# A two-layer gated transformer-like kernel on one core: loads behind the feature stores, an earlier bias split, VectorE steps in another order, and a longer run of filler products

## What is computed

```python
x = x + tanh(g_xattn[0]) * gat2(ctx_512, layernorm(x), W0, a0, b0, W1, a1, b1)
x = x + tanh(g_ffn[0])   * ((silu(n @ gate_w.T * gate_s) * (n @ up_w.T * up_s)) @ down_w.T * down_s)   # n = layernorm(x)
x = x + tanh(g_xattn[1]) * ((1 - gamma) * layernorm(x) + gamma * sym(sigmoid(sim) * top_k_mask(sim)))
x = x + tanh(g_ffn[1])   * sum_over_top2(coef * w2 @ (silu(w1 @ n) * (w3 @ n)))
```

## Time and profile before

| | |
|---|---|
| median of 3 runs | 235.6 us (232.43, 235.60, 235.95) |
| the profiled execution | 235.69 us |
| its span, first to last instruction | 233.9 us |
| mean granted clock of PE, share of full | 0.969 |
| PE busy | 214.0 us, 92% |
| PE weight loads | 164.0 us, 70% |
| VectorE (DVE) busy | 131.9 us, 56% |
| ScalarE (ACT) busy | 85.5 us, 37% |
| POOL busy | 77.8 us, 33% |
| moved by DMA | 26.11 MB |

### The profile page before, as it was taken

One profiled execution on the slowest core, in us unless ns is written; L12 is line 12 of the kernel. 1 busy time (PEld: TensorE's weight loads), 2 busy tenths in 40 slices (PEclk: granted clock), 3 DMA queues, 4 the chain that ended last, 5 costly groups with the idle time before them and its releaser, 6 DMA issues.

```text
span 233.9 us, 3846 instructions
## 1 busy us (share of the span) xinstructions
PE 214.0 (92%) x1290; PEld 164.0 (70%) x1291; DVE 131.9 (56%) x462; ACT 85.5 (37%) x184; POOL 77.8 (33%) x106
## 2 busy tenths in 40 slices
PE   8899979999899979999989999999999999999920
PEld 7486754444487535988969998999999999544510
DVE  0768793758997996898798395851111111536300
ACT  1965434987600246222533245222222222333210
POOL 7704313061001130026450342554456443244320
PEclk9999977999999999999999999999999999999985
DMA  5777229525991014916243223122233312222110
GB/s 143 228 282 234 64 94 332 207 76 218 399 415 62 0 45 135 337 36 198 77 123 118 27 24 34 33 43 45 42 49 93 53 22 30 35 34 34 25 14 7
DMA packets 16107, 26.11 MB, mean 112 GB/s; under 512 B 3894, under 2 KB 11572, under 8 KB 16086
## 3 DMA queue, kind: packets, MB, share of 16 engines
q1 hardware_dynamic: 10774, 19.82, 23.7%
q0 software_dynamic: 3936, 5.64, 13.5%
q10 hardware_dynamic: 1376, 0.39, 0.7%
HBM read 20.73 MB, written 5.51 MB: 112 GB/s over the span
## 4 chain that ended last, share of the span: by engine, by line
PE 60%; DVE 20%; issue 6%; DMA 4%; POOL 3%; ACT 3%; DVEq 0%; POOLq 0%; ACTq 0%
PE PS L2023 21%; PE PS L2047 10%; PE PS L1904 6%; PE PS L1918 5%; PE PS L2063 3%; PE PS L2080 3%; DMA e<-graph_rows,gix 2%; DVE hT L1400 2%; POOL e L648 2%; PE PS L1731 2%; DVE stat L1025 2%; DMA graph_rows<-e 2%; PE PS L1753 2%; PE PS L2056 1%; PE PS L1963 1%
## 5 line engine op out<-in xcount | busy, mean ns | idle before, releaser
L2023 PE MATMUL PS<-hT,e 128*128 128x128 f32 x480 | 58.8, 276 | 0.8 <-ACT hT L931 0.8
L2023 PEld LDWEIGHTS PS<-hT,e 128*128 128x128 f32 x480 | 56.8, 192 | 2.2 <-ACT hT L931 1.5
L1904 PE MATMUL PS<-xnT,e 128*128 128x512 f32 x88 | 40.9, 613 | 2.4 <-DVE hT L1400 1.3
L1651 DVE TENSOR_TENSOR hT<-th,PS 128x512 f32<-128x512 f32 x18 | 12.4, 686 | 45.8 <-PE PS L2023 38.2
L1904 PEld LDWEIGHTS PS<-xnT,e 128*128 128x128 f32 x88 | 16.6, 196 | 22.4 <-issue 19.0
L2047 PE MATMUL PS<-e,hT 128*128 128x256 f32 x120 | 28.6, 381 | 0.2 <-DVE x L1438 0.2
L2047 PEld LDWEIGHTS PS<-e,hT 128*128 128x128 f32 x120 | 21.7, 190 | 3.1 <-issue 0.8
L1918 PE MATMUL PS<-e,hT 128*128 128x256 f32 x96 | 21.9, 383 | 0.0
L687 POOL DMA_INDIRECT out_dram<-a,ids_early x8 | 12.6, 1578 | 27.1 <-ACT a L960 18.0
L632 POOL TENSOR_TENSOR rstd<-veps,nhalf 128x2 f32<-128x2 f32 (+1 forms) x10 | 8.3, 827 | 35.6 <-DVE veps L1034 35.6
L1918 PEld LDWEIGHTS PS<-e,hT 128*128 128x128 f32 x96 | 17.9, 190 | 2.7 <-issue 0.5
(11 more groups left out here) (302 smaller groups left out, 352.7 us busy)
## 6 DMA issues: line engine op xcount, KB each, us to landing
e<-e_in SPq DMA_DIRECT2D x24, 512.0 KB, 6.3
x<-x_in SPq DMA_DIRECT2D x2, 512.0 KB, 5.6
graph_rows<-e SPq DMA_DIRECT2D x4, 256.0 KB, 3.0
out_dram<-x SPq DMA_DIRECT2D x4, 256.0 KB, 2.5
xn_rows<-xn SPq DMA_DIRECT2D x4, 256.0 KB, 2.3
e<-gw_in SPq DMA_DIRECT2D x1, 768.0 KB
e<-uw_in SPq DMA_DIRECT2D x1, 640.0 KB
e<-dw_in SPq DMA_DIRECT2D x1, 640.0 KB
```

Of the source, the lines that this page charges most:

```text
L1651: dve.tensor_tensor(hh[me], th[:, me, :], PS[:, 2 + me, :], ALU.mult).then_inc(gated, 1)
L1904: mm = pe.matmul(PS[:, bank, :], w[:, k, it * P:(it + 1) * P], xnT[:, h, k, :], start=(k == 0), stop=(k == 1))
L2023: mm = pe.matmul(PS[:, bank + q, f * P:(f + 1) * P], w[:, k * F + f * P:k * F + (f + 1) * P], xgT[q][:, k, :], start=(k == 0), stop=(k == 1))
```

## The change

Four edits, in the order of the program:

1. PE_ORDER: the filler between sims(0) and turn_ffn(0) has 13 products in place of 6.
2. DVE_ORDER: hidden_elu(1), which stood whole behind index(0), is cut in its two blocks; one stands between feat_elu(0, 0) and feat_elu(0, 1), the other behind feat_elu(0, 1), ahead of index(0).
3. SP: the transfers of gw, uw, gs and us leave the place ahead of the feature stores and are issued behind the first two of the four stores, just ahead of dw and dsr.
4. POOL: the six instructions of the bias split, with their wait for the bias load, stand ahead of the last constants (from Os on) and no longer behind them. The wait of PE for all constants moves from feat(0, 0) to hot(0), two steps later on PE.

```diff
-                    ("graph_check", 0), ("sims", 0), ("stay_warm", 6, 0), ("turn_ffn", 0), ("turn_ffn", 1), ("sims", 1),
+                    ("graph_check", 0), ("sims", 0), ("stay_warm", 13, 0), ("turn_ffn", 0), ("turn_ffn", 1), ("sims", 1),
...
-            for w, src in ((gw, gw_in), (uw, uw_in)):
-                sp.dma_start(w[:, :, :], src.rearrange("(k p) n -> p k n", p=P)).then_inc(ffn_loaded, 16)
-            for v, src in ((gs, gs_in), (us, us_in)):
-                sp.dma_start(v[:, :], src).then_inc(ffn_loaded, 16)
...
+            def load_up():
+                for w, src in ((gw, gw_in), (uw, uw_in)):
+                    sp.dma_start(w[:, :, :], src.rearrange("(k p) n -> p k n", p=P)).then_inc(ffn_loaded, 16)
+                for v, src in ((gs, gs_in), (us, us_in)):
+                    sp.dma_start(v[:, :], src).then_inc(ffn_loaded, 16)
...
             for b in range(B):
                 if b == 2:
+                    load_up()
                     load_down()
...
             pool.iota(iota_b[:, :], [[1, NL]], base=0, channel_multiplier=0, **small).then_inc(consts, 1)
+            pool.wait_ge(bias_loaded, 16)
+            own(pool.tensor_copy(bias_parts[:, :], bias[:, :]))
+            own(pool.tensor_tensor(bias_rest[:, :], bias[:, :], bias_parts[:, :], ALU.subtract))
+            own(pool.tensor_copy(bias_parts[32:64, :], bias_rest[32:64, :]))
+            own(pool.tensor_copy(bias_parts[64:P, :], bias_rest[64:P, :]))
+            own(pool.tensor_tensor(bias_rest[64:P, :], bias_rest[64:P, :], bias_parts[64:P, :], ALU.subtract))
+            own(pool.tensor_copy(bias_parts[64:P, :], bias_rest[64:P, :]))
+            pool.sem_inc(bias_ready)
             pool.memset(Os[:, :, :, 0:HT - 1], 0.0).then_inc(consts, 1)
...
             pool.wait_ge(consts, CONSTS)
-            pool.wait_ge(bias_loaded, 16)
...
-            pool.tensor_copy(bias_parts[64:P, :], bias_rest[64:P, :]).then_inc(bias_ready, 1)
...
-            def hidden_elu(h):
+            def hidden_elu(h, *parts):
-                for k in range(2):
+                for k in parts or range(2):
...
                 if h == 0 and p == 0:
-                    pe.wait_ge(consts, CONSTS)
...
             def graph_hot(h):
+                if h == 0:
+                    pe.wait_ge(consts, CONSTS)
```

More of the change, by code:

```diff
@@ L432, in build @@
                      ("silu", 5), ("copy_x", 6), ("scale_y", 4), ("silu", 6), ("copy_x", 7), ("scale_y", 5)]
-        DVE_ORDER = [("hidden_elu", 0), ("top", 0), ("hot", 0), ("top", 1), ("feat_elu", 0, 0), ("feat_elu", 0, 1), ("index", 0), ("hidden_elu", 1),
+        DVE_ORDER = [("hidden_elu", 0), ("top", 0), ("hot", 0), ("top", 1), ("feat_elu", 0, 0), ("hidden_elu", 1, 0), ("feat_elu", 0, 1), ("hidden_elu", 1, 1), ("index", 0),
                      ("lead", 0), ("scales", 0), ("flag", 0), ("graph_check", 0),
```

## The result

The changed kernel takes 239.97 us (median of four runs, 239.26 to 241.44), the kernel before 234.01 us beside it (232.17 to 235.95): ratio 1.029, interval 1.017 to 1.041 (the two medians by themselves give 1.025). It is slower, and 3.5 us above the top of the stated range of 231.0 to 236.5; whether by more than 2%, the interval leaves open. The ratios, and the medians from experiment 7 on, leave out every run over 1.5% above its kernel's fastest: single runs that lose another 5 us or so, whatever the cause (238.56 and 238.73 in experiment 8 are such, with a low clock in spite of the filler), and in some lists also runs of the kernel before at 235.2 to 236, so that the ratios of different experiments do not have quite the same base.

The account below looks back on a forecast made before the run. PE was taken as the bound, slowed by a half-clock stretch after a 1.95 us wait for xn. From 235.69 us: -3.3 (clock) + 0.2 (last row later) = 232.6, stated as 232.5; range 231.0 to 236.5.

Parts of the forecast that it names:

- contention term: Last of the four row gathers, now beside the moved loads: 0.6 us slower than its 2.78 us in quiet.
- The FFN loads behind the first two stores: SP's queue: first store lands sooner, gathers start at 19.5 (gain 0.4 us), loads hidden from PE, last row at 27.1.
- rival 2: Loads hold up the gathers: last takes 4.66 us, PE's gap 2.3 us, clock falls; 237.1 us; chance 0.11.
- upper bound of 1.9: Most the loads could add to the last gather, from the first gather's at most 4.66 us beside dw.
- Filler: PE before xn: 13 products (3.47 us) shrink the 1.95 us gap, clock stays full; gain 3.3 us, bounds 0 to 3.3.
- Rival 1: Clock falls all the same: a gap of about 1 us is enough or never the cause; 235.9 us; chance 0.15.
- Bias split: POOL: split ends at 9.2, constants at 11.1, first exponential at 13.3 instead of 12.57, first store issued 0.5 us later.
- VectorE steps: hidden_elu(1) halves ahead of index: gix at 18.65 instead of 17.72, second half's h0T 1.3 us earlier.
- First store: Feature store issued at 15.1, landing in 2.5 to 3.0 us, before gix, so gathers are held by gix.
- FFN loads in time: Loads and gathers, 2.8 MB, end at 28.6 to 30; PE asks at about 32: hidden, 2 us to spare.
- The later part: Everything behind the 31 to 45 us stretch moves along; second-half gathers 3 us earlier than 46.72.
- rival 3: Gathers start when the first store lands, not with gix, 1.7 us earlier with full clock: 230.7 us; chance 0.07.

Follow-up runs that it names:

- experiment 7: Kernel before with 13 filler products and the bias split ahead of the last constants, nothing else: 232.27 us (nine runs, 231.56 to 232.94).
- experiment 8: Kernel before with 13 filler products and the two VectorE steps moved, nothing else: 232.10 us (eight runs, 231.46 to 232.54).
- experiment 3: Kernel before with only the filler changed, 13 products in place of 6: 232.49 us, ratio 0.996.
- experiment 1: Changed kernel with gw, uw, gs and us loaded in their old place, ahead of the feature stores: 231.96 us, ratio 0.994.
- experiment 4: Changed kernel with 28 filler products in place of 13: 234.83 us (234.43 to 235.22).
- experiment 10: Changed kernel with 28 filler products and gw alone (0.79 MB) back ahead of the feature stores: 234.44 us, ratio 1.010.
- experiment 5: Changed kernel, but SP issues the FFN loads only when the four gathered tiles have landed: 240.77 us, ratio 1.037.
- experiment 6: Changed kernel with gw and uw loaded in pieces of 256 columns, 1 KB a row of one packet: 240.19 us, ratio 1.036.

## Why the prediction was wrong

The step that failed is the contention term in "The FFN loads behind the first two stores": "I take 0.6, a third of the way". Measured, the last gather took 6.19 us, 3.4 more than 2.78. The mechanism was named (rival 2); the term for it was mis-sized. The upper bound of 1.9 was wrong as well. It came from the first gather of before, which ran beside dw alone, 0.85 MB, when the change put 2.29 MB there. A bound from a row holds only for the load that the row had. The prediction's own sum stood against its 27.1 as well: it had loads and gathers together, 2.8 MB, end at 28.6 to 30, and in the trace the last bytes of the loads move before 29 and the gathers' before 30.

Point by point:

- **Filler.** Right in mechanism and size: alone it leaves one of two groups of runs, whose medians are 3.3 us apart (3.3 forecast), with the clock full. The four products of sims(1) take 1.99 us in experiment 3, as forecast. 13 products took 3.17 us, not 3.47. In the changed kernel the gap is 3.62 us and the filler saves nothing. Rival 1, that the clock falls anyway, is refuted where the gap is 0 to 0.62 us (the profiles of experiments 1, 3, 4, 7, 8 and 10). No run had a gap near the 1.1 us that the forecast expected for the whole change, so whether the clock would have held there was not tried; the forecast took it for granted.
- **Bias split.** The load was there at 5.06 (5.6 forecast), the split ended at 8.42 (9.2) and the last constant at 10.56 (11.1). ScalarE's sum started at 10.60 instead of 9.95, but the profile shows no wait before it: all of ScalarE's work was 0.46 us later in this execution and ended at 10.52. The forecast mechanism is seen in experiment 1, at about half its size:

```profile
10.80 1.06 ACT L794 ACTIVATE hT<-ctxT 64x1024 f32<-64x1024 f32 x1 [0.65 <-POOL node L619]
```

  No time could be measured for it.
- **VectorE steps.** gix at 18.99 (18.65 forecast) and the order of the steps as forecast. Worth nothing measurable.
- **First store.** Issued at 15.80 (15.1), landed in 2.5 us as forecast, and the gathers were released by gix and not by the store, as forecast, at 20.12 (19.5). The front varies from execution to execution: experiments 4, 5 and 6, with the same code up to the first two stores, issue the first gather at 19.30, 19.01 and 19.79, and the changed kernel at 20.12. In its profiled execution one step of hidden_elu on VectorE took 1.13 us at 8.86, beside POOL's last constants (the split had ended at 8.42), against 0.56 before; in experiment 4 the same step in the same place took 0.42, so neither the split nor the constants explain it.
- **FFN loads in time.** Right: PE never waited for them in the changed kernel. They were hidden from PE; their harm went to a transfer on another queue.
- **The later part.** Right: in the second half the gathers, with no such loads beside them, land in 2.76 us, and everything from there to the end is merely shifted.

The arithmetic closes in the profiled executions of experiment 1 (231.70) and the changed kernel (239.69), 7.99 us apart. The first gather is 0.67 later (20.12 against 19.45), the last takes 3.36 longer (6.19 against 2.83), so xn and turn_ffn are 4.02 later (34.44 against 30.42). By the next bf16 products (45.09 against 37.02) this has grown to 8.07, so the low clock cost 4.05 us. From the forecast: 232.5 + 2.8 (contention) + 0.6 (first gather) + 4.0 (clock) = 239.9.

Rival 2 was the right case. Its place, its mechanism and its point of decision (a gap above 1.95 us) all held; it was priced at 237.1 from the same too narrow bound, and given 0.11. The missing 2.6 us are about 2.1 of a later last row (30.5 instead of 28.4) and 0.7 of a clock that cost 4.05 us and not 3.3. The error is multiplied, since one term decides whether another one falls due: a last row that is later by 3.4 us loses 4 more through the clock. Such a term should have been carried to both sides, with the weight of its uncertainty. In rival 3 the start of 14.85 is neither the 14.61 of before nor the forecast's own 15.1; with 15.1 that case is worth 1.4 us and 231.0. The gathers did not follow the store, so nothing hangs on it.

Two rules of the Trainium skill were weighed. DMA: Bandwidth & Descriptors, "Queues, rings and completion order", has the engines serve their rings in turn; by it a gather should lose a fraction of a microsecond. That size was my own working, for which the section gives no time, and the traces do not bear it out: the first gather's bytes came about 2 us after they were due, and experiment 6, with packets of 1 KB, still took 7.0 us for the last. From 24 us on gathers and loads do move side by side (0.15 MB and 0.57 MB until 26). I leaned on the rule against a row, and that was the wrong way round. What in the path of the gathers holds them (the engines' turns, a queue of descriptors ahead of them, or memory) the runs do not show; they show that the last one pays for the bytes of the loads. TensorE: Matmul & The Clock Gate, "Why this matters for your kernels", asks only for longer gaps to be avoided. Here a gap of 1.95 us came before a fall in the profiled run of the kernel before, whose runs split about evenly between the two levels of time, and filler in that gap removed the split.

What stays open: why the loads alone (238.4 to 238.7) are 1.4 us quicker than the whole change, when they lack the filler. It rests on two runs against four; nothing here tells whether part of it is the front, which varies by 1.1 us between executions.

The version to keep is experiment 1: filler, bias split and VectorE steps, with the loads in their old place, 231.96 us (231.70 to 232.40). It beats the changed kernel by 8.0 us; beside before it is within the noise by the ratio, and lies in the quicker of before's two groups (231.67 to 232.43) with every run. Nearly all of what it gains is the filler; beside the filler alone, measured together with it, it is 0.5 us lower (232.33 to 232.65 there), which the two parts by themselves do not show.

## What to carry to other kernels

Before loads are moved to where "the queue is empty", list every small transfer of every other queue that lands in their shadow and that someone waits for, and price it at the volume that the move puts beside it over the engines' full rate (here 1.44 MB at 415 GB/s = 3.5 us, measured 3.1 to 3.4), not at a share of its own size. Look at the queues one by one, in the kernel as it is, for a stretch in which the small one moves nothing. A bound taken from a row is a bound only for the traffic that stood beside that row. And where a fall of the clock follows a wait of PE, fill the wait with spare products first (here about 3 us in every second run) and then keep the gap short, because a gap of 3.62 us brought the fall back in spite of the filler and cost 4 us on top of the delay.

## What the runs showed of the hardware

- Gathers on POOL's queue issued at 20.12 to 22.99, beside 2.29 MB of loads on SP's queue, moved no byte before 24 us, and the first was due about 2 us earlier; with no loads beside them (experiment 5) all four land within 3.1 us.
- Splitting the loads into packets of 1 KB brought the first gather's rows 5.2 us after its issue instead of 6.3 and did not help the last (7.00 us).
- The clock as against the gap that PE had before, where the gap is read from one profile for each kernel: 0 to 0.62 us, full up to the tail in all six profiles; 1.95 us, low in the profile and in 15 of 31 runs of that kernel by their times; 3.62, 4.42 and 4.79 us (the changed kernel, experiments 6 and 5), low in the profile and in every run. Between 0.62 and 1.95 us there is no row.
- The low stretch lasted 6.8 us behind the gap of 1.95 us and 10.2 us behind each of the gaps of 3.62, 4.42 and 4.79 us, worked out from means of 1 us as above. It did not grow with the gap among those three.
